# Folding the B and C weights into one score projection with dt columns, and new turns, in a fused AdaLN, Mamba-2 and Soft-MoE kernel

## The reference

```python
h = layernorm(x) * (1 + ca) + sa                 # per-batch modulation from silu(c) @ wmod
xn = rmsnorm(h, norm_w)
proj = xn @ in_proj_w.T                          # 772 rows: z 256, x 256, B 128, C 128, dt 4
x_conv = silu(conv_b + 4 causal taps of x_ssm)   # xh: 4 heads of 64
dt = softplus(dt_raw + dt_bias); dA = exp(-exp(A_log) * dt)
h_t = dA * h_{t-1} + (dt * xh)_t B_t^T;  y_t = h_t C_t
y = (y + D * xh) * silu(z);  x = x + ga * (h + y @ out_proj_w.T)
h = layernorm(x) * (1 + cb) + sb                 # then Soft-MoE, 8 experts of 64 slots
logits = rmsnorm(h) . rmsnorm(slot_embeds); dispatch, combine = two softmaxes
x = x + gb * (combine @ experts(dispatch^T @ rmsnorm(h)))
```

## Time and profile before

| | us |
|---|---|
| median of 3 runs | 231.29 |
| lowest, highest | 230.2, 232.47 |
| span of the profiled execution, first to last instruction | 227.2 |
| median less span | 4.1 |

### The profile page before, as it was taken

The page is one execution under the profiler, slowest core; times in us unless marked ns, Lnnn a source line. Parts: engine busy times, 40 slices in busy tenths (PEclk is TensorE's granted clock), DMA queues, the critical chain, the costliest instruction groups (busy, mean ns, idle before and its releaser), DMA issues.

```text
span 227.2 us, 4247 instructions
## 1 busy us (share of the span) xinstructions
PE 205.5 (90%) x1575; PEld 148.2 (65%) x1575; DVE 139.5 (61%) x372; ACT 120.3 (53%) x264; POOL 60.9 (27%) x147
## 2 busy tenths in 40 slices
PE   3879979995799899998978799989999999999995
PEld 2445555673377795475656387765865948659995
DVE  3887868998999956859988875730130221302753
ACT  3879896533468856797531566658327062270000
POOL 6545885016524203984015600000000000000000
PEclk9999999999999999999999999999999999999999
DMA  6404000200600000000500000006222141200122
GB/s 189 118 6 140 1 5 8 87 3 11 197 24 3 0 0 3 1 2 7 183 0 1 0 3 0 0 3 185 49 84 61 42 139 49 85 10 3 46 69 69
DMA packets 15344, 10.72 MB, mean 47 GB/s; under 512 B 1773, under 2 KB 13654, under 8 KB 15326
## 3 DMA queue, kind: packets, MB, share of 16 engines
q1 hardware_dynamic: 15100, 10.31, 15.5%
q10 hardware_dynamic: 226, 0.16, 0.2%
HBM read 9.34 MB, written 1.07 MB: 46 GB/s over the span
## 4 chain that ended last, share of the span: by engine, by line
PE 68%; DVE 11%; ACT 11%; POOL 4%; DMA 3%; issue 2%; ACTq 1%; DVEq 0%; POOLq 0%
PE bank L577 28%; PE bank L922 13%; PE bank L904 11%; PE bank L761 4%; PE bank L814 3%; PE bank L750 2%; POOL root L490 2%; DVE xcT L1309 2%; DVE bst L1183 2%; ACT zsT L1066 2%; PE bank L829 2%; DMA vec_nat<-ffn_slot_norm_gamma_dram 2%; ACT xhT L1072 1%; PE bank L835 1%; PE bank L860 1%
## 5 line engine op out<-in xcount | busy, mean ns | idle before, releaser
L1446 DVE TENSOR_TENSOR eo<-bank,seg_e 128x512 f32<-128x512 f32 x8 | 5.5, 692 | 47.9 <-PE bank L922 47.9
L922 PEld LDWEIGHTS bank<-w_sb,zsT 128*64 128x64 f32 x256 | 27.8, 137 | 3.0 <-issue 3.0
L922 PE MATMUL bank<-w_sb,xcT 128*64 128x128 f32 x256 | 28.8, 273 | 0.0
L922 PE MATMUL bank<-w_sb,zsT 128*64 128x128 f32 x256 | 28.8, 273 | 0.0
L922 PEld LDWEIGHTS bank<-w_sb,xcT 128*64 128x64 f32 x256 | 27.8, 137 | 0.0
L904 PE MATMUL bank<-slotsT,w_sb 128*128 128x512 f32 (+1 forms) x64 | 26.1, 558 | 0.2 <-ACT zsT L1140 0.2
L1140 ACT ACTIVATE zsT<-bank,vecT 128x512 f32<-128x512 f32 x16 | 10.7, 687 | 24.9 <-PE bank L904 24.9
L577 PE MATMUL bank<-xnT,winT 128*128 128x512 f32 x48 | 23.0, 607 | 0.3 <-ACT BT L1053 0.3
L490 POOL TENSOR_TENSOR root<-root,neg_half 128x2 f32<-128x2 f32 (+1 forms) x24 | 20.2, 842 | 2.0
L904 PEld LDWEIGHTS bank<-slotsT,w_sb 128*128 128x128 f32 x64 | 11.4, 190 | 12.6 <-issue 12.1
L1309 DVE SCALAR_TENSOR_TENSOR xcT<-bank,convw,xcT 128x510 f32<-128x510 f32 (+2 forms) x24 | 17.3, 737 | 3.6 <-ACT xcT L1050 3.3
(11 more groups left out here) (165 smaller groups left out, 414.9 us busy)
## 6 DMA issues: line engine op xcount, KB each, us to landing
w_sb<-in_L_ffn_w_dram SPq DMA_DIRECT2D x16, 256.0 KB, 2.9
mods_bc<-mod_dram SPq DMA_DIRECT2D x4, 320.0 KB, 3.5
xin<-in_L_attn_x_dram SPq DMA_DIRECT2D x4, 256.0 KB, 3.1
out_dram<-x1tok SPq DMA_DIRECT2D x16, 64.0 KB, 1.5
mods_bc<-mod_dram SPq DMA_DIRECT2D x4, 192.0 KB, 3.3
seg_e<-mod_dram SPq DMA_DIRECT2D x1, 512.0 KB, 3.8
eo<-in_L_attn_in_proj_w_dram SPq DMA_DIRECT2D x1, 384.0 KB, 4.1
eo<-in_L_wmod_dram SPq DMA_DIRECT2D x1, 256.0 KB, 4.6
```

The source lines that it names most:

```text
L922: q = nc.tensor.matmul(o[j * S:(j + 1) * S, tile_cols(b)], act_h[j][k // 2][:, k % 2, at:at + S], w2_sb[j][:, k, :], start=k == 0 and b == ...
L1446: V.tensor_tensor(o, bank[4 + 2 * (it % 2) + g][:, :].rearrange("p (b d) -> p b d", d=P), b2_bc[:, it, :].unsqueeze(1).broadcast_to((P, 4, ...
```

## The change

- **Scores.** xn C-weights times xn B-weights is xn (Wc^T Wb) xn^T. The setup forms Wc^T Wb (128x128) by one matmul instead of two transposes, with the four dt columns behind it. `project1` makes U = that matrix on xn, first of all; ACT copies it to ut with the scale norm_w (`copy_u`). `scores` multiplies xnT by ut: per batch 260 and 132 columns, where 4 each are dt. The columns of dt in ut are constant (`dt_columns`, POOL, once). C's projection, its copy and the four dt matmuls go.
- **dt** is now read by `dt_in` from gm, after ACT's `copy_scores`, which no longer waits for the convolution: the scores go to banks 4j+3 and 4j+2, and z takes these after the copies.
- **Two banks per instruction.** The banks become one PSUM tensor; `dt_times_x`, `slot_max`, `norm_slots` read two, and `token_max` reads both halves; each waits for both.
- **Space.** mod_rows and sgn_r move into combT; slots and xn2T get tiles of their own.
- **Turns.** All tables of turns are new, on all engines and the DMA queue.

```diff
-            for n in range(ROW_BLOCKS):
-                q = nc.tensor.transpose(bank[1 + n // 4][:, tile_cols(n % 4)], w_nat[:, n, :], ident[:, :])
+            for n in range(2 * CT):
+                nc.tensor.transpose(bank[1][:, tile_cols(n)], w_nat[:, n, :], ident[:, :])
+            mm(bank[2][:, 0:P], w_nat[:, C_BLOCK, :], w_nat[:, B_BLOCK, :])
...
-                for t in range(TP):
-                    q = mm(b3[:, t * H:(t + 1) * H], xnT[j][:, tile_cols(t)], winT[:, DT0:ROWS])
-                q.then_inc(proj_ps[1][j], 1)
+                wait_before(pe, slotsT_done, j, it)
+                mm(b2[:, :], winT[:, U0:U0 + P], xnT[j][:, :]).then_inc(proj_ps[1][j], 1)
...
-                mm(b2[:, :], winT[:, B0:B0 + P], xnT[j][:, :]).then_inc(proj_ps[1][j], 1)
+
+            def scores(j, it):
+
+                wait(pe, ut_done, j, it)
+                if it == 0:
+                    pe.wait_ge(s_ut, j + 1)
+                for bi in range(BP):
+                    o = bank[4 * j + 3 - bi]
+                    mm(o[:, 0:L + H], xnT[j][:, tile_cols(bi * NT)], ut[j][:, bi, :])
+                    mm(o[:, L + H:GW], xnT[j][:, tile_cols(bi * NT + 1)], ut[j][:, bi, P:L + H]).then_inc(g_ps[1][j], 1)
 
             def project2(j, it):
 
-                wait(pe, nabs_done, j, it)
-                mm(bank[4 * j + 3][:, :], winT[:, C0:C0 + P], xnT[j][:, :]).then_inc(proj_ps[1][j], 1)
-                wait(pe, xbc_done, j, it, 3)
-                mm(bank[4 * j + 2][:, :], winT[:, Z0:Z0 + P], xnT[j][:, :]).then_inc(z_ps[1][j], 1)
+                wait(pe, g_done, j, it, 1)
+                mm(bank[4 * j + 3][:, :], winT[:, Z0:Z0 + P], xnT[j][:, :]).then_inc(z_ps[1][j], 1)
...
-            visits = [((0, 6, 53, 56), mean_squares1), ((3, 12, 61, 65), copy_xnT), ((7, 14, 63, 68), exp_dt),
+            visits = [((0, 4, 48, 58), mean_squares1), ((3, 13, 57, 67), copy_xnT), ((12, 19, 66, 74), exp_dt),
...
             def dt_in(j, it):
-                wait(dve, proj_ps, j, it, 1)
+                if it == 0:
+                    dve.wait_ge(s_small, N_SMALL)
                 d = dv[j]
...
+                wait(dve, g_done, j, it)
...
             def slot_max(bi):
                 def visit(j, it):
...
+                    n0 = 4 * j + (0, 2)[bi]
+                    wait(dve, ls_ps, j, it, 2 * bi + 2)
+                    with nc.allow_low_precision("the shift of a softmax"):
+                        V.reduce_max(cshift[j][:, :].rearrange("p (n m) -> p n m", n=2),
+                                     banks[:, n0:n0 + 2, :].rearrange("p n (m t) -> p n m t", m=2), AX.X
+                                     ).then_inc(cshift_done[1][j], 1)
```

More of the change, by code:

```diff
@@ L1396, in visit @@
                 def visit(j, it):
-                    for n in range(NT):
-                        wait(dve, lt_done, j, it, 2 * bi + n + 1)
-                        with nc.allow_low_precision("the shift of a softmax"):
-                            q = V.reduce_max(rshift[j][:, n:n + 1], lt_sb[j][:, n, :], AX.X)
-                    q.then_inc(rshift_done[1][j], 1)
+                    wait(dve, lt_done, j, it, 2 * bi + 2)
+                    with nc.allow_low_precision("the shift of a softmax"):
+                        V.reduce_max(rshift[j][:, :], lt_sb[j][:, :, :], AX.X).then_inc(rshift_done[1][j], 1)
                 return visit
@@ L1441, in _ @@
+            pipeline(dve, visits, once=[(4, vectors), (8, rows_of_mods)])
             dve.wait_ge(s_rows_bc, 48)
```

222 lines of the change are left out of this document (106 added, 116 removed).

## The result

The changed kernel takes 235.78 us (median of 4 runs, 235.3 to 239.78), the kernel before 231.38 (4 runs, 230.2 to 232.47): ratio 1.018, 95% interval 1.0124 to 1.0236. It is slower by about 4 us, where I had forecast 3.3 us faster. Beside the experiments the kernel before had medians of 231.5 to 231.83. Ratios are of fast runs alone, and leave out those over 1.5% above their kernel's fastest (two of them, one of e10 and one of the kernel before, took over 400 us), while the medians given are of all runs.

A forecast was written before the change was run, and what follows sets the result against it. TensorE, busy 90% of the 227.2 us span, was taken as the bound. A lead of 2.8 plus 0.5 us for the gate cut 3.3 us, to 223.9; with 4.1 outside the span, 228.0 us, range 224.0 to 231.5.

The forecast's parts named there:

- PE's work: TensorE's four visits each lose the dt matmuls and C's projection, 1.70 us a visit, 6.8 us in all.
- rival 1: TensorE-bound throughout: the new order fills pass 2's expected holes and all 6.8 us count, 224.5 us; chance 0.22.
- Start: First visit on TensorE: projections start at 13.4 instead of 13.6, no longer behind the out-projection transposes.
- dt's way: First visit: dt_in waits for projection, copy, scores and score copies, running at 19.35, 3.2 us later; convolution at 19.75, before 18.99.
- ACT's order and its tables: ScalarE, pass 1: two more table loads a pass, 5.1 us in all, covered by an earlier chain; first decay 33.4, before 34.62.
- rival 4: Each ScalarE table switch costs another 1.28 us behind the load, 5.1 us more, 233.1 us; chance 0.02.
- The rest of pass 1: After the first decay: pair 0 runs ahead, pair 1 pays, and a lead of 2.6 us remains.
- Rival 2: VectorE sets the time, pass 1's lead is lost and only the gate's 0.5 us remains, 230.8 us; chance 0.21.
- Pass 2: Second pass: TensorE idles about 4.3 us against 0.9, decay 0 at 100.3 against 103.06, lead stays 2.7 to 2.9.
- Two banks: Merged VectorE instructions save 0.5 us a pass but wait for both banks; taken as 0, ends -1.0 and +1.5 us.
- Gate ahead of x1: Tail of pass 2 on VectorE: pair 0's gate(1) goes before pair 1's x1(0), shrinking a 1.3 us hole by 0.5.
- Rival 3: ScalarE's inner Exp loads between Silus cost 2.07 us a pass if its chain starts no earlier, 235.4 us; chance 0.08.

The follow-up runs named there:

- e10: The changed kernel with its two-bank VectorE instructions split again to one bank each: 236.41 us, ratio 1.0194 to the kernel before.
- e2: The changed kernel with useless bf16 products filling TensorE's holes in the setup and both passes: 233.2 us, ratio 1.0068 to the kernel before.
- e4: The changed kernel with only the 3 useless products in the setup: 236.89 us, ratio 1.0147 to the kernel before.
- e5: The changed kernel with pair 1's softplus moved behind POOL's basis and gate-weight products of pair 0 in pass 2: 234.4 us, ratio 1.0135.
- e18: The kernel before with token_max, slot_max and norm_slots reading two banks per instruction, all else as before: 232.08 us, ratio 1.0026.
- e14: The changed kernel with useless bf16 products in TensorE's three holes of pass 2 only: 234.06 us, ratio 1.0111 to the kernel before.
- e1: The changed kernel with Silu in place of Exp in pair 1's exp_dt, so the four inner table loads go: 236.18 us, ratio 1.0194.
- e3: The kernel before with pair 1's exp_dt moved behind both Silus of pair 0's z in both passes, adding four table loads: 242.48 us, ratio 1.046.

## Why the prediction was wrong, by its steps

**The sum.** Its last term, 4.1 us outside the span, is wrong: time less span is some 2.0 in the runs that list both, and the rest was the short profiled run. The median on which it was put is right, so the forecast of 228.0 does not move.

**PE's work, right as work.** The matmuls went as said (x1575 to x1535), but "PE busy falls by about 6.8 us" did not come: 206.0 against 205.5. I had no term for the clock; the profile before shows 1.00 in every stretch. An estimate: a mean clock of 0.978 over 233.6 us, with 0.5 as the lower level, is about 5 us of added busy time, and the setup's slow products (9.14 to 13.84, before 8.81 to 11.48) are 2.0 more, together about the 7.3 that are missing. PE's holes in the two passes are 20.1 us, before 14.3; they did not fill, so rival 1 fails.

**Start.** I put the projections at 13.4; they begin at 15.25, since PE's setup products took 2.07 us instead of 1.13. The profile's granted clock is 1.00 there, so why is open; with the holes of the setup filled they took 1.13 again (e2, e4). The start counts: e5's, 1.25 earlier, reached pass 2 whole. It is a term of the sum that was mis-sized by 1.85 us.

**dt's way, right in size in pass 1.** dt_in runs at 21.25 instead of 19.35, and 1.85 of the 1.90 are the late start. In pass 2 I did not walk it: dt_in waits 4.29 us on DVE and runs at 91.02 against 85.46 before.

**ACT's order and its tables.** From the first Silu load the durations fit: the Exp load comes 5.09 us behind it (5.0 foreseen), each load is 1.28 and the next row 0.02 later, so rival 4 fails as said. The load came at 22.38, and the first decay at 37.05 instead of 33.4: 1.73 of the 3.65 come from the start, the other 1.9 stand around z of pair 1, whose products took 3.63 instead of 1.94 after a hole of 2.54 on PE, and for which ACT waited. Of "ACT's chain starts 5 us sooner" 3.5 came.

**The rest of pass 1, right as far as known.** The lead of 2.6 us was to be there at the start of pass 2. Against the profile from which I forecast it is not (84.71 against 84.47); against the trace of e18 it is 2.95 (87.66). In size this is luck in part: the start came late and the first decay too, and pass 1 made up for both in ways that I had not worked out. Rival 2, the lead of pass 1 lost, is at least not what made the kernel slower.

**Pass 2, the step that failed.** "Scores of pair 1 end 91.8 ... decay 0 at 100.3": they end at 98.03 and the decay is at 106.81. I took the lead of pass 1 and moved everything by it, without walking PE's new order. That order puts the transposes of xn of pair 1 behind scores and fill_slots, at 91.28 (before 84.03). PE is busy without a hole from 84.71 to 98.03, 13.32 us against 13.08 before: what the visits lost in products is filled with other work. Pair 1's dt, now behind its copied scores, comes at 99.49 instead of 91.69 on DVE and its convolution at 99.78 instead of 93.01, and the running sums of pair 1 (105.30, before 101.61), its parts and its Silu then hold pair 0 up in three queues. I had written down that PE would idle there and that the segment products wait behind pair 1's running sums, and had priced this at 4.3 us of holes that cost nothing. Measured, the stretch from there to y_of(0) is 6.3 us longer: 1.9 by the clock (e14), 4.4 by the waits.

**Two banks.** 0 was right within what can be measured (e10, e18); a merged maximum takes 1.219, as estimated.

**Gate ahead of x1.** Together with all else behind y_of(0): -0.35 against -0.5.

**The rivals.** Rival 3 forecast 235.4 and its sign, for a first load later than 21.9 (it came at 22.38), but its mechanism is refuted by e1: without the inner loads nothing is gained. Its price, 2.07 a pass, came from idle time alone; e3 shows what the same loads cost in the old order, 5.5 a pass with the lower clock behind them. Right number, wrong reason.

**What is settled:** the large loss lies between running sums and y_of(0) of pair 0 in pass 2; about 1.7 us of the median are TensorE's lower clock there; the inner loads and the two-bank instructions are not the cause, and POOL's order is at most 0.5 us. The new structure in the old order costs 11 us, of which dt's way 4.4 and the bank of the running sums 2.9; the new turns take back 6.7, all of it in pass 1, and make the stretch of pass 2 longer.

**Not settled:** which order would free pair 0 at the new turns (three limits stand abreast). That pair 1's late work ahead of pair 0's makes the remaining 4.4 us is read from the chain of waits: no run that moved it won them back. Open too are the last 3.5 us at the old turns, with their low clock, and the setup's slow products. No version here beats the kernel before.

## What to carry to other kernels

Work taken from the busiest engine pays only where nothing else must pass through what replaces it: here 6.8 us of matmuls went, and a value that every later step needs (dt) was put behind a copy, a product and another copy. A forecast can also be off by the run that it was read from: here one short profile hid 2 to 3 us of pass 1. Before you forecast a new order, walk it on every queue up to the first result that both visits wait for, the second pass too, and look for the younger visit standing ahead of the older. Price a hole of TensorE also with the work behind it at half speed, and when a move gains nothing, look in the profile for the second wait that was hidden behind the first.
